# A two-layer decoder on one core: cross attention's outputs in 32-wide strips, the convolution's bias as bf16 rows, one-operation clamps

## The reference

```python
x = _layernorm(x + _L0_attn_ref(x, ...))         # self attention, 16 heads of 8, relative positions
x = _layernorm(x + _L0_xattn_ref(x, ctx, ...))   # cross attention, 16 heads of 64
x = _layernorm(x + _L0_ffn_ref(x, ...))          # 8 experts, top 2, the eighth passes its input through
x = _layernorm(x + _L1_attn_ref(x, ...))         # retention with decay, gates, its own layer norm
x = _layernorm(x + _L1_xattn_ref(x, ctx, ctx, ...))   # cross attention, 16 heads of 8
x = _layernorm(x + _L1_ffn_ref(x, ...))          # quantized linear, conv of 3 taps, silu, quantized linear
```

```python
# _L0_xattn_ref
sim = jnp.einsum('bihd,bjhd->bhij', q, k) * SCALE
attn = jax.nn.softmax(sim, axis=-1)
out = jnp.einsum('bhij,bjhd->bihd', attn, v)      # d = 64
return out.reshape(B, N, INNER) @ Wo              # INNER = 1024
# _L1_attn_ref
g = jax.nn.sigmoid((x @ g_w.T + g_b).reshape(b, t, h, r))
# _L1_ffn_ref
h = bit_linear(x, w1)
h = depthwise_conv1d(h.transpose(0, 2, 1), conv_w, conv_b)   # 512 channels, bias conv_b
h = jax.nn.silu(h.transpose(0, 2, 1))
return bit_linear(h, w2)
```

## Time and profile before

| | us |
|---|---|
| runs | 916.98, 922.15, 922.53 |
| median | 922.15 |
| profiled execution, time | 916.87 |
| profiled execution, span | 915.1 |
| TensorE busy | 753.2 (82%) |
| VectorE busy | 565.2 (62%) |
| ScalarE busy | 402.5 (44%) |
| GpSimd busy | 215.2 (24%) |
| mean granted clock of TensorE | 0.941 of full |

### The profile page before, as it was taken

One profiled execution on the slowest core, in us unless ns is written; L12 is line 12 of the kernel. 1 busy time (PEld: TensorE's weight loads), 2 busy tenths in 40 slices (PEclk: granted clock), 3 DMA queues, 4 the chain that ended last, 5 costly groups with the idle time before them and its releaser, 6 DMA issues.

```text
span 915.1 us, 21252 instructions
## 1 busy us (share of the span) xinstructions
PE 753.2 (82%) x8906; PEld 552.4 (60%) x8906; DVE 565.2 (62%) x1520; ACT 402.5 (44%) x1026; POOL 215.2 (24%) x215
## 2 busy tenths in 40 slices
PE   3679999999999799999876675789888888988874
PEld 2346666767666577666665473666666665766541
DVE  0046665556666766666663733687788887788722
ACT  1345444555544455444443111354554554454521
POOL 6201111100111261111013103233333333332200
PEclk9989999999999899999988795899999999999965
DMA  8614424234443234442322110000000000000000
GB/s 338 228 47 142 142 96 139 74 119 142 141 142 130 104 98 141 141 139 102 118 88 87 52 44 20 7 8 10 14 15 11 10 11 10 14 11 4 5 4 6
DMA packets 48271, 72.16 MB, mean 79 GB/s; under 512 B 2880, under 2 KB 43328, under 8 KB 45488
## 3 DMA queue, kind: packets, MB, share of 16 engines
q1 hardware_dynamic: 45248, 63.37, 20.2%
q0 software_dynamic: 2352, 5.18, 2.5%
q10 hardware_dynamic: 576, 2.24, 0.7%
HBM read 32.32 MB, written 38.47 MB: 77 GB/s over the span
## 4 chain that ended last, share of the span: by engine, by line
PE 57%; DVE 20%; ACT 9%; issue 6%; POOL 4%; DMA 3%; POOLq 0%; SPq 0%; DVEq 0%; ACTq 0%
PE bank L466 52%; PE bank L523 4%; POOL kbd L457 3%; DVE sc L1104 2%; DVE nmxa L1108 2%; DVE sc L1111 2%; DVE nmb L1153 1%; DVE q L1412 1%; DVE scol L1399 1%; DMA row_sb<-rows 1%; ACT kbd L1048 1%; ACT kbd L1047 1%; ACT nmT L939 1%; DVE q L1148 1%; ACT kbd L1043 1%
## 5 line engine op out<-in xcount | busy, mean ns | idle before, releaser
L403 POOL TENSOR_TENSOR rext<-rext,ones 128x1008 f32<-128x1008 f32 x16 | 29.8, 1865 | 323.8 <-ACT rext L897 323.8
L949 ACT ACTIVATE pTb<-bank 77x512 f32<-77x512 f32 x128 | 66.7, 590 | 4.3 <-PE bank L466 4.3
L939 ACT ACTIVATE nmT<-bank 128x128 f32<-128x128 f32 x32 | 8.9, 278 | 125.8 <-PE bank L587 71.8
L1104 DVE TENSOR_TENSOR sc<-bank,rel 128x512 f32<-128x512 f32 x64 | 41.1, 683 | 32.4 <-PE bank L466 32.1
L1153 DVE TENSOR_REDUCE nmb<-bank 128x4 f32<-128x308 f32 x128 | 53.5, 470 | 9.8 <-PE bank L466 9.7
L1368 DVE TENSOR_TENSOR k<-bank,k_sb 128x512 f32<-128x512 f32 x64 | 41.2, 686 | 27.5 <-PE bank L466 27.2
L466 PE MATMUL bank<-wa,qa 32*128 32x512 f32 (+1 forms) x160 | 45.6, 609 | 10.4 <-ACT rext L897 6.1
L466 PE MATMUL bank<-k,xdT 128*128 128x512 f32 x96 | 50.1, 662 | 0.0
L419 POOL DMA_INDIRECT xg_dram<-x_all,to_slot x32 | 31.2, 975 | 79.8 <-DVE wpass L1262 71.0
L457 POOL TENSOR_SCALAR kbd<-kbd 128x512 f32<-128x512 f32 x16 | 30.7, 1920 | 80.1 <-ACT kbd L1043 80.1
L466 PE MATMUL bank<-nmT,k_sb 32*77 32x128 f32 x1024 | 47.6, 279 | 0.0
(11 more groups left out here) (266 smaller groups left out, 1837.3 us busy)
## 6 DMA issues: line engine op xcount, KB each, us to landing
rel_dram<-rext SPq DMA_DIRECT2D x16, 2040.0 KB, 6.4
rel<-rel_dram SPq DMA_DIRECT2D x16, 960.0 KB, 5.5
rext<-w_up SPq DMA_DIRECT2D x1, 1792.0 KB, 9.9
rel<-w_down SPq DMA_DIRECT2D x1, 1792.0 KB, 8.4
wb<-w_b SPq DMA_DIRECT2D x1, 1604.0 KB, 16.4
xT_ld<-xT SPq DMA_DIRECT2D x16, 64.0 KB, 6.3
x_all<-x ACTq DMA_DIRECT2D x1, 1024.0 KB, 10.7
wl<-w_l SPq DMA_DIRECT2D x1, 1024.0 KB, 18.2
```

The costliest lines, as they stand in the source:

```text
L949: A.activation(dst[0:C, 4 * i:4 * i + 4, :], bank[b][0:C, :].rearrange("p (a i) -> p a i", a=4), ACT.Exp).then_inc(exped["b"], 1)
L1104: added = mark(V.tensor_tensor(sc[:, part[i], :], bank[2 * j + i][:].rearrange("p (a j) -> p a j", a=4), rel[:, t % 2, part[i], :], ALU.add))
```

## The change

Cross attention of the first stage: one set of sums for all heads, each head's sums 32 wide in one of four strips of a bank (b_sm0, b_sm1), and the values in two 32-wide halves for each head, four strips side by side (b_v0, b_v1); one pair of Ln and Exp over 512 columns instead of two; the products take each sum twice; the rows of the output projection are laid out anew on the host ("cross"). The convolution's bias: onesrow is all ones and cbrow bf16; the bias is loaded into 32 partitions, split on VectorE into three bf16 parts in rows 0 to 2, the rest zero, by one scaling, two multiply-adds and three conversions (two back and forth, one at the end) with the table "third". Its load moves from GpSimd's queue to SyncE's. Both clamps keep only the minimum; the 1 is added inside ScalarE's Ln as its bias. ORDER1 and ORDER2 are written anew for all engines. The diff, without lines that only adapt counts of semaphores and tables:

```diff
...
@@ -70,23 +70,25 @@
-    "pe": ("r_rank:-3 a_s b_x:-1 b_q:-1 b_s0:-1 b_s1:-1 b_st0:-1 b_nm:-1 b_st1:-1 a_t0 a_t1 b_inj:-1 a_t2 a_t3 "
-            "a_qkv:2 a_v b_v0:-1 b_v1:-1 rel01:2 a_out b_out:-1 rel_last:2 rel23:2 v0 b_r:-1 b_lg:-1").split(),
-    "dve": ("b_norm:-2 a_ln:-1 rel_last:1 v0:-1 b_lg:-2 r_c:-3 a_m0 b_qhi:-1 b_m0:-1 b_m1:-1 b_m2:-1 b_m3:-1 "
-            "a_m1 r_a:-2 a_t1 a_t3 r_b:-2 a_qkv:2 a_div b_u0:-1 b_u1:-1 a_out b_out:-1").split(),
-    "act": ("b_qlo:-1 b_nm:-1 a_e0 a_e1 a_t0 a_e2 a_e3 r_a:-2 a_t2 a_qkv:2 b_e0:-1 b_e1:-1 b_e2:-1 b_e3:-1 a_v "
-            "b_r0:-1 b_r1:-1 rel01:2 a_ln b_ln:-1 rel23:2 b_r:-1 v0 b_x").split(),
-    "pool": "rel_fill:2 r_send:-2".split(),
-    "sp": "load_rel:1 store_rel:2".split(),
+    "pe": ("b_lg:-2 r_rank:-3 a_s b_x:-1 b_q:-1 b_s0:-1 b_s1:-1 b_st0:-1 a_t0 b_nm:-1 b_st1:-1 a_t1 b_inj:-1 "
+            "a_t2 a_t3 a_qkv:2 a_v b_sm0:-1 b_sm1:-1 b_v0:-1 b_v1:-1 rel01:2 a_out b_out:-1 rel23:2 v0 b_r:-1 "
+            "rel_last:2").split(),
+    "dve": ("v0:-1 b_lg:-2 r_c:-3 a_m0 b_qhi:-1 b_m0:-1 b_m1:-1 b_m2:-1 b_m3:-1 a_m1 r_a:-2 a_t1 a_t3 r_b:-2 "
+            "a_qkv:2 a_div b_u0:-1 b_u1:-1 a_out b_out:-1 b_norm:-1 a_ln rel_last:2").split(),
+    "act": ("b_nm:-1 a_e1 a_t0 a_e2 a_e3 a_t2 r_a:-2 b_e0:-1 b_e1:-1 b_e2:-1 b_e3:-1 a_qkv:2 a_v b_rc:-1 "
+            "rel01:2 b_ln:-1 a_ln rel23:2 b_r:-1 v0 b_x b_qlo a_e0:1").split(),
+    "pool": "rel_fill:2 r_send:-14".split(),
+    "sp": "store_rel:2 load_rel:2".split(),
-    "pe": ("f_turn:-2 e_out:-1 f_down:-2 e_x d_qk:1 e_q d_gv:1 e_s d_rank:1 f_x:-1 f_up:-1 e_nm d_s01:1 e_st "
-            "d_s3:1 e_inj d_v:1 d_out:1 e_v v1:1 d_x:2").split(),
-    "dve": ("d_ln2:2 d_m2 d_m3 f_silu:-2 f_quant:-2 d_out c_norm:1 d_ln v1 e_div:-1 d_norm e_out:-1 f_down:-2 "
-            "e_norm:-1 d_rope:1 f_in:-1 e_m0 e_m1 e_m2 e_m3 d_qk:1 c_sum:2 f_norm:-2 d_m0:1 d_m1:1").split(),
-    "act": ("f_turn:-2 e_ln:-1 e_x f_ln:-2 e_q d_gates:1 f_x:-1 d_sig:1 e_nm f_exp:-1 c_ln:2 f_sig:-1 e_e0 e_e1 "
-            "d_v:1 e_e2 e_e3 d_ln:1 e_v d_ln2:1 d_x:2").split(),
-    "pool": "gather:2 d_res d_gate e_res:-1 d_fade f_clamp:-2".split(),
+    "pe": ("e_out:-1 e_x f_down:-2 d_qk:1 e_q d_gv:1 e_s d_rank:1 f_x:-1 f_up:-1 e_nm d_s01:1 e_st d_s3:1 "
+            "e_inj d_v:1 d_out:1 e_v d_x:2 v1:1 f_turn:-1").split(),
+    "dve": ("d_m2:-1 d_m3:-1 f_silu:-3 f_quant:-3 d_out:-1 c_norm d_ln:-1 d_ln2:2 e_div:-2 v1:-1 d_norm:-1 "
+            "e_out:-2 f_down:-3 e_norm:-2 d_rope f_in:-2 e_m0:-1 f_norm:-3 e_m1:-1 e_m2:-1 e_m3:-1 d_qk c_sum:1 "
+            "d_m0 d_m1").split(),
+    "act": ("e_ln:-1 e_q d_gates:1 f_ln:-2 f_x:-1 d_sig:1 f_exp:-1 e_nm c_ln:2 f_sig:-1 e_e0 e_e1 d_v:1 e_e2 "
+            "e_e3 d_ln:1 e_v d_ln2:1 f_turn:-1 d_x:2 e_x:1").split(),
+    "pool": "d_fade gather:2 f_clamp:-2 e_res:-1 d_res:1 d_gate:1".split(),
@@ -238,8 +240,10 @@
-        onesrow = sb("onesrow", [32, P])
-        cbrow = sb("cbrow", [32, HID])
+        onesrow = sb("onesrow", [32, P], BF16)
+        cbrow = sb("cbrow", [32, HID], BF16)
+        cbias = scd[0:32, 0:4, :].rearrange("p h t -> p (h t)")
+        cpart = scd[0:32, 4:6, :].rearrange("p h t -> p (h t)").bitcast(BF16)
@@ -352,6 +356,7 @@
+            sp.dma_start(cbias, conv[3:4].partition_broadcast(32)).then_inc(ld_conv, 16)
@@ -381,14 +386,10 @@
-            G.memset(onesrow[:], 0.0).then_inc(pre_pool, 1)
-            pool.wait_ge(pre_pool, 7)
-            G.memset(onesrow[0:1, :], 1.0).then_inc(pre_pool, 1)
-            G.memset(cbrow[:], 0.0).then_inc(pre_pool, 1)
+            G.memset(onesrow[:], 1.0).then_inc(pre_pool, 1)
-            pool.wait_ge(pre_pool, 10)
-            G.dma_start(cbrow[0:1, :], conv[3:4]).then_inc(st_zero, 16)
+            pool.wait_ge(pre_pool, 8)
...
@@ -446,7 +447,7 @@
-                G.tensor_scalar(eg, eg, EXP_MAX, 1.0, ALU.min, ALU.add).then_inc(d_gate1, 1)
+                G.tensor_scalar(eg, eg, EXP_MAX, None, ALU.min).then_inc(d_gate1, 1)
@@ -454,7 +455,7 @@
-                G.tensor_scalar(he, he, EXP_MAX, 1.0, ALU.min, ALU.add).then_inc(f_e1, 1)
+                G.tensor_scalar(he, he, EXP_MAX, None, ALU.min).then_inc(f_e1, 1)
...
@@ -610,18 +611,31 @@
                 pe.wait_ge(nm_sb, t + 1)
                 less_max((bank[6], bank[7], bank[4], bank[5]), turned)
 
+            def at_key(h):
+
+                return 8 * (h // 8) + 4 * (h % 2) + h % 8 // 2
+
+            def b_sums_(j):
+
+                def f(t):
+                    pe.wait_ge(exped["b"], 4 * t + 2 + 2 * j)
+                    for u in (2 * j, 2 * j + 1):
+                        for s in range(4):
+                            last = mm(bank[7][strip(s), u * P:(u + 1) * P], ones[0:C, 0:32],
+                                      pTb[0:C, at_key(4 * u + s), :])
+                    last.then_inc(sums["b"], 1)
+                return f
+
             def b_values(j):
+
                 def f(t):
                     pe.wait_ge(exped["b"], 4 * t + 2 + 2 * j)
-                    for c in range(4):
-                        for i in range(2):
-                            last = mm(bank[5 if j else 7][half(i), c * P:(c + 1) * P], ones[0:C, 0:XH],
-                                      pTb[0:C, 8 * j + 4 * i + c, :])
-                    last.then_inc(sums["b"], 1)
-                    for c in range(4):
-                        for i in range(2):
-                            last = mm(bank[4 if j else 6][half(i), c * P:(c + 1) * P], v0[0:C, 8 * j + 2 * c + i, :],
-                                      pTb[0:C, 8 * j + 4 * i + c, :])
+                    for u in range(2):
+                        for v in range(2):
+                            for s in range(4):
+                                h = 4 * (2 * j + u) + s
+                                last = mm(bank[4 if j else 6][strip(s), (2 * u + v) * P:(2 * u + v + 1) * P],
+                                          v0[0:C, h, 32 * v:32 * v + 32], pTb[0:C, at_key(h), :])
                     last.then_inc(values["b"], 1)
                 return f
 
@@ -673,7 +687,8 @@
-                "b_st1": b_turn(1), "b_inj": b_inj, "b_v0": b_values(0), "b_v1": b_values(1), "b_out": b_out,
+                "b_st1": b_turn(1), "b_inj": b_inj, "b_sm0": b_sums_(0), "b_sm1": b_sums_(1),
+                "b_v0": b_values(0), "b_v1": b_values(1), "b_out": b_out,
...
@@ -950,13 +964,11 @@
-            def b_recips(j):
-                def f(t):
-                    act.wait_ge(sums["b"], 2 * t + j + 1)
-                    part = rb[:, 4 * j:4 * j + 4, :]
-                    step(A.activation(part, bank[5 if j else 7][:].rearrange("p (c i) -> p c i", c=4), ACT.Ln))
-                    A.activation(part, part, ACT.Exp, scale=-1.0).then_inc(recips["b"], 1)
-                return f
+            def b_recips(t):
+                act.wait_ge(sums["b"], 2 * t + 2)
+                part = rb[:, 0:4, :]
+                step(A.activation(part, bank[7][:].rearrange("p (c i) -> p c i", c=4), ACT.Ln))
+                A.activation(part, part, ACT.Exp, scale=-1.0).then_inc(recips["b"], 1)
@@ -982,7 +994,7 @@
-                "b_r0": b_recips(0), "b_r1": b_recips(1), "b_ln": deviation("b"), "v0": v0_,
+                "b_rc": b_recips, "b_ln": deviation("b"), "v0": v0_,
@@ -1031,7 +1043,7 @@
-                step(A.activation(eg, eg, ACT.Ln))
+                step(A.activation(eg, eg, ACT.Ln, bias=1.0))
...
@@ -1156,11 +1168,13 @@
 
             def b_mul(j):
                 def f(t):
-                    part = slice(4 * j, 4 * j + 4)
-                    dve.wait_ge(recips["b"], 2 * t + j + 1)
+                    dve.wait_ge(recips["b"], t + 1)
                     dve.wait_ge(values["b"], 2 * t + j + 1)
-                    V.tensor_tensor(oTb[:, part, :], bank[4 if j else 6][:].rearrange("p (c i) -> p c i", c=4),
-                                    rb[:, part, :], ALU.mult).then_inc(oT_ready["b"], 1)
+                    V.tensor_tensor(
+                        oTb[:, 4 * j:4 * j + 4, :].rearrange("p (u v) i -> p u v i", u=2),
+                        bank[4 if j else 6][:].rearrange("p (u v i) -> p u v i", u=2, v=2),
+                        rb[:, 2 * j:2 * j + 2, :].unsqueeze(2).broadcast_to([P, 2, 2, P]), ALU.mult
+                        ).then_inc(oT_ready["b"], 1)
                 return f
 
             def v0_(t):
...
@@ -1304,7 +1318,14 @@
-            dve.wait_ge(ld_conv, 16)
+            dve.wait_ge(ld_conv, 32)
+            step(V.tensor_scalar(cbias, cbias, const("third", 0, 1)[0:32, :], None, ALU.mult))
+            for i in (1, 2):
+                step(V.tensor_copy(cpart, cbias))
+                step(V.scalar_tensor_tensor(out=cbias, in0=cpart, scalar=const("third", i, i + 1)[0:32, :], in1=cbias,
+                                            op0=ALU.mult, op1=ALU.add))
+            V.tensor_copy(cbrow[:], cbias).then_inc(w_ready, 1)
...
@@ -1478,6 +1500,8 @@
+    cross = np.arange(H * XH).reshape(4, 4, 2, XH // 2).transpose(0, 2, 1, 3).reshape(-1)
```

(2 more changed lines are left out.)

18 lines of the change are left out of this document (9 added, 9 removed).

## The result

The changed kernel takes 888.44 us (median of 4 runs, 885.95 to 894.26) against 920.84 us (4 runs, 916.98 to 922.53): a ratio of 0.966, 95% interval 0.960 to 0.9725. The forecast was 887 us, with 875 to 900 as its range. The sum came out near. Two of its three parts did not: the first stage gave far less than forecast, the second far more.

A forecast was written before the change was run, and what follows sets the result against it. No engine is full, so waits decide: TensorE's gapless stretch in the first stage, a latency loop in the second. -16.7 + 4.5 - 19.8 = -32.0 us from 916.87 gives 884.9; forecast 887 us, range 875 to 900.

The forecast's parts named there:

- Cross attention's matmuls: First stage, 16 tiles: sums and values as 32-wide matmuls four abreast, 0.87 us less each, 13.9 us in all.
- The first stage's order: First stage, TensorE: rel_last moved behind b_r fits an idle gap, saving 2.8 us; the other moves, scatters included, 0.
- Between the stages: Ahead of the experts: VectorE's bias split adds 3.3 us and a lower clock 1.2 us, +4.5 us in the sum.
- the whole 3.7 us: First up projection: by the clock rule its first 3.7 us would be doubled; the forecast took a third, +1.2 us.
- The second stage's loop: Feed-forward chain: silu starts 7.2 us after f_up's start instead of 8.17; -1.0 us a tile, -14 us over 14 periods.
- The tail: Last two f_up, alone at 1.2 GHz: bias, clamp and f_exp's place save 2.4 us each, 4.8 us together.
- E: Cross attention's strips don't run four abreast, +1.8 us a tile; 930 us, slower; chance 0.03.
- F: Second stage: GpSimd's gathers hold the clamp; with 6.5 us for the pair, 935 us; chance 0.02.
- D: The pause between the stages keeps the clock low through the experts, +12 to +24 us, 899 to 911; chance 0.04.
- B: Second stage's loop closes through masks, e_st and attention values; silu gains only 0.3 us; 897 us; chance 0.16.
- C: Second stage's e_st isn't held, silu gains 1.3 us, and the clock doesn't fall between the stages; 874 to 878 us; chance 0.05.
- A: The forecast itself: both stages shorten, with e_st held by the later maxima's copy; 878 to 895 us; chance 0.70.

The follow-up runs named there:

- The changed kernel with halves: The changed kernel with its cross attention's outputs and sums back in two 64-wide halves, changed orders, bias and clamps kept: 892.82 us, ratio 0.972.

## Why the prediction was right, and where it was not

- **Cross attention's matmuls.** 3.65 to 2.73 us, forecast 2.8; 1.02 us a tile by the strips in the new order (0.75 in the old), forecast 0.87. The failed step is the factor: "16 x 0.87". In rounds 8, 9 and 14 the period grew, by 1.6, 3.2 and 4.2 us, and the first stage gave 1.8 us, outside the bounds of -12 to -19. The condition that the saving holds "as long as the engines behind it keep up" was the right question, asked of the wrong side: it was the supply ahead of TensorE that did not keep up (rounds 8 and 14), and VectorE's picks (part of round 9; 1.7 of its 3.2 us come without the strips, and their cause is open). The "stall" of 1.0 us in round 9 was in the trace of before; I had followed an undisturbed period and multiplied it.
- **The first stage's order.** rel_last stands in the gap ahead of the router's logits, as forecast. The changed kernel with halves has a period of 26.18 instead of 26.45: 0.27 a tile for all of the new order (0.2 forecast for rel_last; no run moves it alone). The scatters' place costs nothing either way, as forecast.
- **Between the stages.** +4.7, forecast +4.5; 3.3 of VectorE's work and 1.4 of a lower clock. The first up projection takes 5.10 us instead of 3.69. The clock is 0.50 up to 523 us, 0.74 to 525 and 1.00 behind. The Trainium skill, TensorE: Matmul & The Clock Gate, Part 1, says that activity releases the throttled state; the trace agrees. But the whole 3.7 us that the prediction drew from that rule did not come.
- **The second stage's loop.** Every event came within 0.35 us of its forecast: exponential T+3.20 (3.1), clamp T+4.01 (4.1), e_st T+4.04 (4.1), d_s3 T+5.11 (5.4), silu T+6.88 (7.2). The masks end last, as forecast, and by 0.15 us only. Their bound was set too late by the distance from e_st to d_s3: 1.07 us, where I kept the old 1.35. The bf16 bias held TensorE 0.32 us, where I took 0.21. The clamp took 1.49 us, between my 1.26 and the 1.93 of two operations. The 0.77 us that the Trainium skill, GPSIMD Engine Reference, 3.1, gives for 512 elements in a tight loop isn't reached here. What follows silu shrank too, by 0.25 us, where I gave it 0.05; no run says why. So -1.54 a tile where -1.0 was forecast, beyond the bound of -1.3. The undone parts price it at 0.74 (bias), 0.47 (clamps) and 0.33 (the rest, which is the orders). The 14 periods gave 22.9 us instead of 14.
- **The tail** (from f_up of the last tile but one) gave 5.5 us for 4.8.
- **The sum** was right by luck, by two misses of opposite sign: 15 us too much in the first stage, 9 too little in the second. Of the prediction's rivals E and F are out by the first rows of the new profile, D by the clock (1.00 from 525 us on) and B by its size: the masks do end last, but silu gained 1.29 us and not 0.3. Of C silu's gain of 1.3 came, though e_st was held as in A, and the clock fell all the same.

## What to carry to other kernels

A saving read from one period holds only for the periods that look like it: list all periods of before, and ask of each odd one which other input comes last there. Count instructions as well as time: shorter matmuls in greater number can run ahead of their own instruction supply, above all right behind a large transfer, and the pause then costs the clock too. Work that prepares an operand belongs where its engine idles, not ahead of a copy that TensorE waits for.

## What the runs showed of the hardware

- TensorE's instructions come in packets of 16.4 KB on a DMA queue, 256 instructions each. Runs of 128 passes in 3.6 us outran them, for up to 2.8 us at packet boundaries, in all ten profiled executions of kernels with the strips and separate sums; the value runs with halves, with 5.5 us for as many, have no pause in either of two.
- In all 38 breaks the matmul behind it starts 2.2 to 2.7 us after the transfer of a packet began.
- The same pause after pass 59 of tile 7 was followed by a granted clock of 0.50 in five executions (pauses of 0.80 to 0.90 us, round 8 takes 28.0 to 28.1 us) and by no fall in two (0.85 and 0.91 us, 26.4 and 26.5 us). Its length alone does not tell whether the clock falls.
- Four matmuls of 512 columns in four 32-wide strips take 0.86 us, as long as sixteen of 128.
- GpSimd's one-operation clamp of 128x512 takes 1.49 us, its two-operation one 1.93.
- On the other chip, all four kernels show TensorE waiting 1 to 5 us at a time in round 14, around the load of rel and of the weights, at matmuls for which the profile mostly shows no cause; ScalarE too sits idle 8.3 us there. No instruction packet's transfer begins in the 5 us before the longest of these waits ends, so it is another kind of wait than above. The cause stays open.
